# The high-by-low product of the scores as two 64-row matmuls on the two halves of the array

## The chip, the cores and the metric

The kernel runs on one core of a Trainium2 chip. The metric is the device time of one execution, in microseconds (us). The time before is 4194.33 us, the median of three runs (4191.17 to 4195.89).

## What is computed

A layer norm, a ReLU, and a masked attention with 8 heads of 64 columns over 1024 nodes, for 16 images; the input is added at the end. In the reference:

```python
h = jnp.maximum(_layernorm(x, axis=-1), 0.0)          # x: 16 x 1024 x 512, adj: 1024 x 1024
q = (h @ Wq + bq).reshape(b, n, H, HD)                # H = 8, HD = 64; k and v likewise
scores = jnp.einsum('bihd,bjhd->bhij', q, k) / jnp.sqrt(jnp.float32(HD))
mask = jnp.where(adj == 0, jnp.float32(-1000000000.0), jnp.float32(0.0))
weights = jax.nn.softmax(scores + mask[None, None, :, :], axis=-1)
out = x + jnp.einsum('bhij,bjhd->bihd', weights, v).reshape(b, n, H * HD)
```

## The kernel before

Every engine has its own program, written out by hand, and semaphores tie them together. The outer loop runs over 16 images (the first and the last are written out, the 14 between are a hardware loop). In an image, the heads come in 4 pairs; a pair has 32 **units**, a head 16. A unit u takes one column block of 128 keys for a group of 4 row blocks of 128 queries. On TensorE a unit turns 4 blocks of probabilities into PSUM tile T (`turn_probs`, 4 transposes) and multiplies the turned block u-2 by v into O (`contract`, 2 matmuls). On every even unit it also computes one **score block**, 5 blocks ahead (`score`): 128 queries by 1024 keys into S, of which there are two. Image by image that makes 64 score blocks and 128 units.

ScalarE takes T to pT's high part (`probs_hi`), VectorE subtracts for the low part (`probs_low`), for every unit. For every score block VectorE adds the mask and takes the maximum (`shift`, 1024 columns), ScalarE takes the exponential (`exponential`).

All matmuls in float32r drop low bits, so each operand is held as a high and a low part, and a product has three terms. For the scores, the parts of q stand one under the other: for the first head of a pair rows 0 to 63 of qA hold q_high, rows 64 to 127 q_low; for the second head (qB) it is the other way round. k has two planes of 1024 columns, [k_high; k_high] and [k_low; k_low], both with the same 64 rows twice. A score block is then, for each of the two halves of 512 columns, two matmuls over all 128 rows: q times plane 0 (L513) and q times plane 1 (L514). So the second one computes q_high k_low and, along with it, q_low k_low. The second copy of the 64 rows of k comes by DMA (`copy_k`, L233).

Other work is put into given units of the program (the **slots**): the projection of q and k of the next pair, eight pieces of 6 matmuls (L483) at u = 4, 6, 8, 9, 12, 14, 16, 17 of each pair; v of the next image, 12 matmuls each (L496), at u = 121, 123 to 127 and in the first units of the next image; the turning of the next image's normalised input, 4 transposes (L462), at u = 83, 85, 87, 88, 91, 92, 95, 96; and the turning of the output of a group, 4 transposes (L546), at every eighth unit. ScalarE and VectorE take these results from the PSUM bank misc and split them (L654, L664, L772; L669, L762). The first score block of the next pair stands at u = 22.

GpSimd makes k_low (L390), normalises the input tiles (L371) and finishes the outputs: `finish` reads yparts, a copy of misc that ScalarE makes (`copy_y`, L624), and adds to xres.

SyncE issues all DMAs from one queue, in program order, with its waits in between: in every pair the stores and loads of xres, `copy_k` of the first 512 columns, input tiles (xln), `copy_k` of the other 512 columns, the load of the next 1 MB of weights (wqk, L222), and in the third pair of an image behind that six input tiles (L214), each of which waits for the turning of the tile two before it.

Of the kernel before, what the change touches and what calls it, by code (L numbers as in the profile page):

```python
# [81 lines left out]
def some(n):  # L82

    return not (isinstance(n, int) and n <= 0)


def adj_preln_kernel(nc, x, adj, Wq, bq, Wk, bk, Wv, bv, out):
    with ExitStack() as ctx:
# [28 lines left out]
        yparts = sb("yparts", [P, GB, 2, HD])  # L117
# [45 lines left out]
        q_low, k_low, k_copied = sem("q_low"), sem("k_low"), sem("k_copied")  # L163
        v_mm, v_biased, v_hi, v_ready = sem("v_mm"), sem("v_biased"), sem("v_hi"), sem("v_ready")
# [11 lines left out]
        def qk_buffers(pair, second):  # L176


            if not second:
                return qA[:, :], kA[:, :, :]  # L180
            return qB[:, pair % 2, :], kB[:, pair % 2, :, :]

# [27 lines left out]
        def _(sp):  # L210
# [14 lines left out]
            def copy_k(b, p, half):  # L225

                cols = slice(half * HALF, (half + 1) * HALF)

                sp.wait_ge(k_low, 4 * (PAIRS * b + p) + 2 * (half + 1))
                for second in range(2):  # L230
                    _, k = qk_buffers(p, second)
                    own, other = (slice(0, HD), slice(HD, P))[::-1 if second else 1]
                    sp.dma_start(k[other, :, cols].bitcast(F32), k[own, :, cols].bitcast(F32)  # L233
                                 ).then_inc(k_copied, 16)

# [35 lines left out]
            for half in range(2):  # L271
                copy_k(0, 0, half)
            store_wqk(3)
# [11 lines left out]
            def body(b, first=False, last=False):  # L285
                for p in range(PAIRS):
# [24 lines left out]
                    if not (last and p == PAIRS - 1):  # L311
                        copy_k(b, p + 1, 0)
                    if p < len(STATS_SLOTS) and not last:
                        for t in STATS_TILES[p][2:]:
                            sp.wait_ge(bn_done, NB * (b + 1) + t - XLN + 1)
                            load_xln(b + 1, t)
# [5 lines left out]
                    if not (last and p == PAIRS - 1):  # L322
                        copy_k(b, p + 1, 1)
                    if not (last and p >= PAIRS - 2):

                        sp.wait_ge(qk_mm, 4 * (PAIRS * b + p + 1) + 4)
                        load_wqk((p + 2) % PAIRS)
                    if p == len(STATS_SLOTS) - 1 and not last:
                        for t in range(XLN, NB):
                            sp.wait_ge(h_turned, NB * (b + 1) + t - XLN + 1)  # L330
                            load_xln(b + 1, t)
# [123 lines left out]
        def _(pe):  # L455
# [44 lines left out]
            def score(b, s):  # L500
# [6 lines left out]
                pe.wait_ge(k_copied, 64 * (pair + 1))  # L507
                if some(n - 1):
                    pe.wait_ge(exped, n - 1)
                for half in range(2):  # L510
                    cols = slice(half * HALF, (half + 1) * HALF)
                    dst = S[:, s % 2, cols]
                    pe.matmul(dst, q[:, i * P:(i + 1) * P], k[:, 0, cols], start=True, stop=False)  # L513
                    mm = pe.matmul(dst, q[:, i * P:(i + 1) * P], k[:, 1, cols], start=False, stop=True)  # L514
# [96 lines left out]
        def _(act):  # L611
            def copy_out(b, g):
                n = GROUPS * b + g
                act.wait_ge(contracted, NB * (n + 1))
                if some(n):
                    act.wait_ge(o_turned, n)
                act.copy(oT[:], O[:]).then_inc(o_copied, 1)

            def copy_y(b, g):
                n = GROUPS * b + g  # L620
                act.wait_ge(o_turned, n + 1)
                if some(n):
                    act.wait_ge(y_added, n)
                act.copy(yparts[:].rearrange("p i l d -> p (i l d)"), misc[:]).then_inc(y_copied, 1)  # L624
# [268 lines left out]
```

## Time and profile before

| | |
|---|---|
| median of three runs | 4194.33 us |
| the profiled execution: its span | 4186.6 us |
| PE / PEld (matmuls / weight loads) busy | 97% / 81% |
| DVE / ACT / POOL busy | 75% / 75% / 31% |
| granted TensorE clock, mean | 0.998 |

The median is 7.7 us over the span of the profiled execution, which covers the first to the last instruction of the program. "Busy" of a matmul is longer than what it keeps from the next one: matmuls follow each other before the one ahead has ended, so that the distances between starts, in the timeline, are what counts.

### The profile page before, as it was taken

Reading aid. Unit: us, or ns where it says so; the run is one execution under the profiler, and the core shown is the slowest. Engines: PE = TensorE matmul, PEld = TensorE weight load, DVE = VectorE, ACT = ScalarE, POOL = GpSimd, SP = SyncE. Lnnn points to the kernel's source line nnn. Section 1 sums busy time; section 2 is a strip of 40 time slices with the busy share of each in tenths; the row PEclk is TensorE's granted clock in tenths of the full one; section 3 lists DMA queues with packets and bytes.
Section 4 is the critical chain, followed back from the end, with each engine's and each line's share of the span. In section 5 each row is a group of like instructions: output and inputs, shape, how many; then the busy total and the mean of one; then the engine's idle time right before and its main releaser. Section 6 shows DMA issues by size and latency. Waiting matters only on the chain.

```text
span 4186.6 us, 77847 instructions
## 1 busy us (share of the span) xinstructions
PE 4080.4 (97%) x22528; PEld 3370.6 (81%) x22528; DVE 3120.0 (75%) x5128; ACT 3149.6 (75%) x5642; POOL 1287.4 (31%) x1665
## 2 busy tenths in 40 slices
PE   7999999999999999999999999999999999999998
PEld 6888888888787887878878788788887888888887
DVE  6877868778687786777867677676777768767677
ACT  5877868778687786867868688686886868868687
POOL 4233332333323333223333233332332322333222
PEclk9999999999999999999999999999999999999999
DMA  5221212212222221122212122121221212212111
GB/s 176 72 73 56 81 48 75 66 57 83 61 60 67 65 77 59 59 67 76 66 59 71 54 76 66 59 79 47 76 72 54 82 48 71 83 44 83 46 51 31
DMA packets 219598, 282.56 MB, mean 67 GB/s; under 512 B 12305, under 2 KB 143377, under 8 KB 210577
## 3 DMA queue, kind: packets, MB, share of 16 engines
q1 hardware_dynamic: 219152, 277.14, 21.9%
q8 instruction: 217, 3.56, 0.4%
q14 instruction: 229, 1.87, 0.2%
HBM read 172.23 MB, written 37.75 MB: 50 GB/s over the span
## 4 chain that ended last, share of the span: by engine, by line
PE 89%; DVE 4%; issue 3%; ACT 2%; DMA 1%; POOL 1%; DVEq 0%; SPq 0%; POOLq 0%; ACTq 0%
PE O L538 21%; PE T L525 19%; PE misc L483 17%; PE S L513 10%; PE S L514 10%; PE misc L496 8%; PE misc L546 3%; DVE pT L796 2%; PE misc L462 1%; ACT pT L633 1%; DVE qA L772 1%; DMA xln<-in_x 1%; ACT qA L664 1%; DVE S L790 1%; DVE hT L762 0%
## 5 line engine op out<-in xcount | busy, mean ns | idle before, releaser
L796 DVE TENSOR_TENSOR pT<-T,pT 128x512 fp32r<-128x512 f32 x2048 | 1412.4, 690 | 831.1 <-ACT pT L633 808.8
L633 ACT CAST pT<-T 128x512 fp32r<-128x512 f32 x2048 | 1192.7, 589 | 711.0 <-PE T L525 676.1
L538 PE MATMUL O<-pT,vs 128*128 128x512 f32 x4096 | 1366.0, 415 | 60.0 <-DVE pT L796 46.0
L790 DVE CUSTOM_DVE_ANT_0 S<-S,mask 128x1024 f32<-128x1024 f32 x1024 | 1252.3, 1223 | 5.9 <-PE S L514 4.3
L525 PEld LDWEIGHTS T<-ident,probs 128*128 128x128 f32 x8192 | 1013.9, 140 | 258.4 <-ACT probs L641 0.3
L525 PE MATMUL T<-ident,probs 128*128 128x128 f32 x8192 | 1210.1, 272 | 0.0
L641 ACT ACTIVATE probs<-S,negmax 128x1024 f32<-128x1024 f32 x1024 | 1152.6, 1126 | 8.5 <-DVE negmax L790 5.3
L538 PEld LDWEIGHTS O<-pT,vs 128*128 128x128 f32 x4096 | 690.9, 189 | 178.2 <-DVE pT L796 70.4
L483 PE MATMUL misc<-hT,wqk 128*128 128x512 f32 x3036 | 789.1, 395 | 0.0
L483 PEld LDWEIGHTS misc<-hT,wqk 128*128 128x128 f32 x3036 | 560.6, 188 | 120.3
L400 POOL TENSOR_TENSOR yparts<-yparts 128x256 f32<-128x256 f32 x256 | 188.7, 737 | 1043.9 <-ACT yparts L624 1043.2
L513 PE MATMUL S<-kA,qA 128*128 128x512 f32 x1024 | 447.2, 437 | 3.9 <-ACT probs L641 3.2
L513 PE MATMUL S<-kB,qB 128*128 128x512 f32 x1024 | 447.0, 436 | 0.0
L514 PE MATMUL S<-kA,qA 128*128 128x512 f32 x1024 | 403.3, 394 | 0.0
L514 PE MATMUL S<-kB,qB 128*128 128x512 f32 x1024 | 402.3, 393 | 0.0
L496 PE MATMUL misc<-wv,hT 128*128 128x512 f32 x1476 | 363.8, 395 | 0.4 <-issue 0.4
L377 POOL TENSOR_TENSOR vs<-proj,vs 128x512 fp32r<-128x512 f32 x128 | 168.2, 1314 | 543.4 <-ACT vs L679 543.4
L496 PEld LDWEIGHTS misc<-wv,hT 128*128 128x128 f32 x1476 | 271.2, 188 | 65.8 <-issue 6.5
L654 ACT ACTIVATE proj<-misc,bqk 128x512 f32<-128x512 f32 x253 | 174.4, 689 | 182.7 <-PE misc L483 182.7
L390 POOL TENSOR_TENSOR kA<-proj,kA 64x512 fp32r<-64x512 f32 x128 | 164.5, 1285 | 474.9 <-ACT kB L664 474.9
L513 PEld LDWEIGHTS S<-kA,qA 128*128 128x128 f32 x1024 | 193.9, 189 | 27.2 <-issue 5.7
L514 PEld LDWEIGHTS S<-kA,qA 128*128 128x128 f32 x1024 | 195.2, 191 | 21.4
(68 smaller groups left out, 3333.0 us busy)
## 6 DMA issues: line engine op xcount, KB each, us to landing
wqk<-wqk_split SPq DMA_DIRECT2D x63, 1024.0 KB, 7.0
xln<-in_x SPq DMA_DIRECT2D x240, 256.0 KB, 3.7
xres<-in_x SPq DMA_DIRECT2D x66, 512.0 KB, 3.7
kA<-kA SPq DMA_DIRECT2D x128, 256.0 KB, 3.2
kB<-kB SPq DMA_DIRECT2D x128, 256.0 KB, 3.7
out<-xres SPq DMA_DIRECT2D x64, 512.0 KB, 3.2
probs<-in_adj SPq DMA_DIRECT2D x4, 1024.0 KB, 5.1
wqk_split<-vs SPq DMA_DIRECT2D x3, 1024.0 KB, 11.0
```

The source lines that it names most:

```text
L400: gp.tensor_tensor(y, y, yparts[:, :, 1], ALU.add).then_inc(y_summed, 1)
L483: mm = pe.matmul(bank, wqk[:, w, c, wl, :], hT[:, hl, c, cols], start=n == 0, stop=n == len(parts) - 1)
L496: mm = pe.matmul(bank, hT[:, hl, c, j * P:(j + 1) * P], wv[:, wl, c, :], start=n == 0, stop=n == len(parts) - 1)
L513: pe.matmul(dst, q[:, i * P:(i + 1) * P], k[:, 0, cols], start=True, stop=False)
L514: mm = pe.matmul(dst, q[:, i * P:(i + 1) * P], k[:, 1, cols], start=False, stop=True)
L525: mm = pe.transpose(T[:, u % 2, i * P:(i + 1) * P], probs[:, (GB * g + i) % RING, j * P:(j + 1) * P], ident[:])
L538: mm = pe.matmul(O[:], vs[:, j, head, :], pT[:, u % PT, part, :], start=(j == 0 and part == 0), stop=(j == NB - 1 and part == 1))
L633: act.copy(pT[:, u % PT, 0, :], T[:, u % 2, :]).then_inc(p_hi, 1)
L641: act.activation(probs[:, s % RING, :], S[:, s % 2, :], ACT.Exp, bias=negmax[:, s % RING:s % RING + 1], scale=-1.0, accum_out=rowsum[:, s ...
L654: act.activation(proj[:, k % 2], bank, ACT.Identity, bias=bqk[:, w, p % PAIRS:p % PAIRS + 1], scale=-SCALE if w == 0 else 1.0).then_inc(qk ...
L790: dve.tensor_tensor_reduce(S[:, s % 2, :], S[:, s % 2, :], mask[:, s % NB, :], 1.0, 3.0e38, ALU.add, ALU.min, negmax[:, s % RING:s % RING ...
L796: dve.tensor_tensor(pT[:, u % PT, 1, :], T[:, u % 2, :], pT[:, u % PT, 0, :].bitcast(F32), ALU.subtract).then_inc(p_lo, 1)
```

## The change

1. For each score block the two matmuls q times plane 0 stay as they are, now both in front. In place of the two 128-row matmuls q times plane 1 stand two matmuls over 64 rows, q_high times k_low: for columns 0 to 511 on rows 0 to 63, for columns 512 to 1023 on rows 64 to 127 (two halves of the array, two PSUM banks). The product q_low k_low is no longer computed.
2. The half that lies on the rows on which q_high does not stand needs a copy of q_high there. `copy_q` makes it by DMA in four pieces of 64 x 512 for every pair: for row blocks 0 to 3 into the plane-1 rows of k that became free, for row blocks 4 to 7 into a new tile, qdup.
3. `copy_k` leaves out the copies of plane 1 that nobody reads: two of its four DMAs in a pair carry one plane, two carry both.
4. qdup gets its room from yparts, which is now the tile oT: `copy_out` (O to oT) waits until GpSimd has finished with the group before (y_added), not for the turning alone.
5. `score` waits for three of the four q copies too; for the last one (second head, row blocks 4 to 7) only where it is read. That copy waits, on SyncE, for the pair's last score block, and the other waits of copy_q are on ScalarE's high parts.

On TensorE a score block and what surrounds it, in the first image. Before (S is the tile of scores, T of turned probabilities, O of the contraction):

```order
L525 MATMUL T<-ident,probs 128x128 x4
L538 MATMUL O<-pT,vs 128x512 x2
L525 MATMUL T<-ident,probs 128x128 x4
L513 MATMUL S<-kB,qB 128x512
L514 MATMUL S<-kB,qB 128x512
L513 MATMUL S<-kB,qB 128x512
L514 MATMUL S<-kB,qB 128x512
L483 MATMUL misc<-hT,wqk 128x512 x6
```

The same place now:

```order
L573 MATMUL T<-ident,probs 128x128 x4
L586 MATMUL O<-pT,vs 128x512 x2
L573 MATMUL T<-ident,probs 128x128 x4
L555 MATMUL S<-kB,qB 128x512 x2
L562 MATMUL S<-kB 128x512
L562 MATMUL S<-kB,qB 128x512
L522 MATMUL misc<-hT,wqk 128x512 x6
```

The number of matmuls is the same; the two of plane 0 stand together, and the two of L562 are the 64-row ones (the sizes printed are those of the output).

On SyncE's queue, the third pair of an image in the loop, from the second half of the k copies on. Before:

```order
L233 DMA kA<-kA 64x2x512 [waits k_low]
L233 DMA kB<-kB 64x2x512
L222 DMA wqk<-wqk_split 128x2048 [waits qk_mm]
L214 DMA xln<-in_x 128x512 [waits h_turned] x6
L239 DMA out<-xres 128x8x128 [waits y_added]
```

Now:

```order
L247 DMA kA<-kA 64x2x512 [waits k_low]
L247 DMA kB<-kB 64x512
L256 ISA
L265 DMA qdup<-qA 64x512 [waits qk_high]
L235 DMA wqk<-wqk_split 128x2048 [waits qk_mm]
L256 REGISTER_ALU
L264 REGISTER_ALU [waits qk_high]
L265 DMA qdup<-qB 64x512 [waits scored]
L227 DMA xln<-in_x 128x512 [waits h_turned] x6
```

The load of the weights stands behind the copy out of qA and its wait, and the six input tiles behind the copy out of qB with two waits.

The diff:

```diff
--- before.py
+++ after.py
@@ -114,7 +114,8 @@
         bv_all = sb("bv_all", [P, D])
         bqk = sb("bqk", [P, 2, PAIRS])
         ident = sb("ident", [P, P])
-        yparts = sb("yparts", [P, GB, 2, HD])
+        yparts = oT[:].rearrange("p (i l d) -> p i l d", i=GB, l=2)
+        qdup = sb("qdup", [P, HALF], F32R)
         negmax = sb("negmax", [P, RING])
         rowsum = sb("rowsum", [P, 2 * RING])
         rinv = sb("rinv", [P, 2, GB])
@@ -161,6 +162,7 @@
         h_turned, h_hi, h_lo = sem("h_turned"), sem("h_hi"), sem("h_lo")
         qk_mm, qk_evac, qk_high = sem("qk_mm"), sem("qk_evac"), sem("qk_high")
         q_low, k_low, k_copied = sem("q_low"), sem("k_low"), sem("k_copied")
+        q_copied, q_copied_last = sem("q_copied"), sem("q_copied_last")
         v_mm, v_biased, v_hi, v_ready = sem("v_mm"), sem("v_biased"), sem("v_hi"), sem("v_ready")
         scored, shifted, exped = sem("scored"), sem("shifted"), sem("exped")
         turned, p_hi, p_lo, contracted = sem("turned"), sem("p_hi"), sem("p_lo"), sem("contracted")
@@ -179,6 +181,17 @@
             if not second:
                 return qA[:, :], kA[:, :, :]
             return qB[:, pair % 2, :], kB[:, pair % 2, :, :]
+
+        def q_again(pair, second, i):
+
+
+            rows = slice(HD, P) if not second else slice(0, HD)
+            at = i % GB * P
+            if i >= GB:
+                return qdup[rows, at:at + P]
+            _, k = qk_buffers(pair, second)
+            at += HALF if second else 0
+            return k[rows, 1, at:at + P]
 
         def x_tile(b, t):
 
@@ -230,8 +243,27 @@
                 for second in range(2):
                     _, k = qk_buffers(p, second)
                     own, other = (slice(0, HD), slice(HD, P))[::-1 if second else 1]
-                    sp.dma_start(k[other, :, cols].bitcast(F32), k[own, :, cols].bitcast(F32)
+                    planes = slice(0, 2 if half != second else 1)
+                    sp.dma_start(k[other, planes, cols].bitcast(F32), k[own, planes, cols].bitcast(F32)
                                  ).then_inc(k_copied, 16)
+
+            def copy_q(b, p, second, half):
+
+
+                pair = PAIRS * b + p
+                q, k = qk_buffers(p, second)
+                own, other = (slice(0, HD), slice(HD, P))[::-1 if second else 1]
+                sp.wait_ge(qk_high, 2 * (4 * pair + 2 * half + 1) + 1 + second)
+                sp.sem_inc(sp_passed)
+                src = q[own, half * HALF:(half + 1) * HALF]
+                if half == 0:
+                    dst = k[other, 1, second * HALF:(second + 1) * HALF]
+                else:
+                    dst = qdup[other, :]
+                    if second and some(pair):
+                        sp.wait_ge(scored, 16 * pair)
+                sp.dma_start(dst.bitcast(F32), src.bitcast(F32)
+                             ).then_inc(q_copied_last if second and half else q_copied, 16)
 
             def store(b, p):
                 sp.sem_inc(sp_passed)
@@ -270,6 +302,8 @@
             store_wqk(2)
             for half in range(2):
                 copy_k(0, 0, half)
+                for second in range(2):
+                    copy_q(0, 0, second, half)
             store_wqk(3)
             store_wqk(0)
             sp.wait_ge(h_turned, NB)
@@ -310,6 +344,8 @@
                                 load_xres(b, p + 1)
                     if not (last and p == PAIRS - 1):
                         copy_k(b, p + 1, 0)
+                        for second in range(2):
+                            copy_q(b, p + 1, second, 0)
                     if p < len(STATS_SLOTS) and not last:
                         for t in STATS_TILES[p][2:]:
                             sp.wait_ge(bn_done, NB * (b + 1) + t - XLN + 1)
@@ -321,10 +357,13 @@
                             load_xln(b + 1, t)
                     if not (last and p == PAIRS - 1):
                         copy_k(b, p + 1, 1)
+                        copy_q(b, p + 1, 0, 1)
                     if not (last and p >= PAIRS - 2):
 
                         sp.wait_ge(qk_mm, 4 * (PAIRS * b + p + 1) + 4)
                         load_wqk((p + 2) % PAIRS)
+                    if not (last and p == PAIRS - 1):
+                        copy_q(b, p + 1, 1, 1)
                     if p == len(STATS_SLOTS) - 1 and not last:
                         for t in range(XLN, NB):
                             sp.wait_ge(h_turned, NB * (b + 1) + t - XLN + 1)
@@ -505,13 +544,22 @@
                 pair = PAIRS * b + s // 16
                 pe.wait_ge(q_low, 4 * pair + 3 + (s // 8) % 2)
                 pe.wait_ge(k_copied, 64 * (pair + 1))
+                pe.wait_ge(q_copied, 48 * (pair + 1))
+                second = (s // 8) % 2
+                if second and i >= GB:
+                    pe.wait_ge(q_copied_last, 16 * (pair + 1))
                 if some(n - 1):
                     pe.wait_ge(exped, n - 1)
                 for half in range(2):
                     cols = slice(half * HALF, (half + 1) * HALF)
-                    dst = S[:, s % 2, cols]
-                    pe.matmul(dst, q[:, i * P:(i + 1) * P], k[:, 0, cols], start=True, stop=False)
-                    mm = pe.matmul(dst, q[:, i * P:(i + 1) * P], k[:, 1, cols], start=False, stop=True)
+                    pe.matmul(S[:, s % 2, cols], q[:, i * P:(i + 1) * P], k[:, 0, cols],
+                              start=True, stop=False)
+                for half in range(2):
+
+
+                    cols, rows = slice(half * HALF, (half + 1) * HALF), slice(half * HD, half * HD + HD)
+                    q_hi = q[rows, i * P:(i + 1) * P] if half == second else q_again(s // 16, second, i)
+                    mm = pe.matmul(S[:, s % 2, cols], q_hi, k[rows, 1, cols], start=False, stop=True)
                 mm.then_inc(scored, 1)
 
             def turn_probs(b, u):
@@ -610,18 +658,17 @@
         @block.scalar
         def _(act):
             def copy_out(b, g):
+
                 n = GROUPS * b + g
                 act.wait_ge(contracted, NB * (n + 1))
                 if some(n):
-                    act.wait_ge(o_turned, n)
+                    act.wait_ge(y_added, n)
                 act.copy(oT[:], O[:]).then_inc(o_copied, 1)
 
             def copy_y(b, g):
                 n = GROUPS * b + g
                 act.wait_ge(o_turned, n + 1)
-                if some(n):
-                    act.wait_ge(y_added, n)
-                act.copy(yparts[:].rearrange("p i l d -> p (i l d)"), misc[:]).then_inc(y_copied, 1)
+                act.copy(oT[:], misc[:]).then_inc(y_copied, 1)
 
             def probs_hi(b, u):
                 n = UNITS * b + u
```

## Rows read from the trace of the kernel before

**Rows 1.** The head of the page: the span, each engine's busy time and number of instructions.

```profile
span 4186.6 us, 77847 instructions
PE 4080.4 (97%) x22528; PEld 3370.6 (81%) x22528; DVE 3120.0 (75%) x5128; ACT 3149.6 (75%) x5642; POOL 1287.4 (31%) x1665
```

**Rows 2.** The page's chain of work that ended last, by engine.

```profile
PE 89%; DVE 4%; issue 3%; ACT 2%; DMA 1%; POOL 1%; DVEq 0%; SPq 0%; POOLq 0%; ACTq 0%
```

**Rows 3.** Groups by form, the whole program: count, busy us, mean ns, idle before.

```profile
L514 PE MATMUL S<-kA,qA 128*128 128x512 f32 x1024 | 403.3, 394 | 0.0
L514 PEld LDWEIGHTS S<-kA,qA 128*128 128x128 f32 x1024 | 195.2, 191 | 21.4
```

**Rows 4.** Timeline of PE, one score block: start us, duration us.

```profile
2003.37 0.48 PE L513 MATMUL S<-kA,qA 128*128 128x512 f32 x1
2003.69 0.40 PE L514 MATMUL S<-kA,qA 128*128 128x512 f32 x1
2003.92 0.39 PE L513 MATMUL S<-kA,qA 128*128 128x512 f32 x1
2004.15 0.39 PE L514 MATMUL S<-kA,qA 128*128 128x512 f32 x1
2004.38 0.62 PE L538 MATMUL O<-pT,vs 128*128 128x512 f32 x2
```

**Rows 5.** Timeline of PEld, the weight loads of the same block.

```profile
2003.35 0.19 PEld L513 LDWEIGHTS S<-kA,qA 128*128 128x128 f32 x1
2003.46 0.19 PEld L514 LDWEIGHTS S<-kA,qA 128*128 128x128 f32 x1
2003.69 0.19 PEld L513 LDWEIGHTS S<-kA,qA 128*128 128x128 f32 x1
```

**Rows 6.** Busy us of each engine in five stretches of one image.

```profile
core 0: us, PE busy (x) PEld busy (x) DVE busy (x) ACT busy (x) POOL busy (x), PEclk, DMA share, GB/s
1979.25:1986.58 7.33, 6.62 (x41) 5.36 (x40) 5.43 (x7) 6.58 (x12) 2.67 (x4) 1.00 0.67 211
1992.04:2003.37 11.33, 11.33 (x71) 9.59 (x70) 10.14 (x18) 9.86 (x19) 2.10 (x3) 1.00 0.01 1
2007.00:2037.05 30.05, 30.05 (x165) 25.04 (x164) 21.80 (x37) 22.81 (x41) 10.71 (x15) 1.00 0.25 71
2044.98:2065.16 20.18, 19.45 (x125) 16.10 (x124) 19.20 (x35) 17.39 (x32) 6.70 (x9) 1.00 0.22 71
2109.36:2138.94 29.58, 28.58 (x144) 23.06 (x142) 15.32 (x26) 12.56 (x23) 8.51 (x8) 1.00 0.01 3
```

**Rows 7.** Timeline of PE at a pair's end: its wait, the next pair's first block.

```profile
1984.35 0.60 PE L525 MATMUL T<-ident,probs 128*128 128x128 f32 x4
1985.66 0.73 PE L538 MATMUL O<-pT,vs 128*128 128x512 f32 x2 [0.71 <-DVE pT L796]
1986.58 0.48 PE L513 MATMUL S<-kA,qA 128*128 128x512 f32 x1
```

**Rows 8.** ACT's last high part for that block, and landings of DMAs (page).

```profile
1981.84 0.62 ACT L664 CAST qA<-proj 64x512 fp32r<-64x512 f32 x1
...
wqk<-wqk_split SPq DMA_DIRECT2D x63, 1024.0 KB, 7.0
...
kA<-kA SPq DMA_DIRECT2D x128, 256.0 KB, 3.2
```

**Rows 9.** Timelines at the end of an image's third pair: SP, ACT, PE, POOL, PE.

```profile
2038.78 0.67 SPq L222 DMA_DIRECT2D wqk<-wqk_split  x1
...
2040.67 0.34 SPq L214 DMA_DIRECT2D xln<-in_x  x1
...
2039.64 0.62 ACT L664 CAST qA<-proj 64x512 fp32r<-64x512 f32 x1
...
2041.95 0.40 PE L514 MATMUL S<-kB,qB 128*128 128x512 f32 x1
...
2046.66 1.52 POOL L371 TENSOR_SCALAR xln<-xln,negmean,rstd 128x512 f32<-128x512 f32 x2 [3.33 <-DMA xln<-in_x]
...
2047.49 0.66 PE L462 MATMUL misc<-ident,xln 128*128 128x128 f32 x4 [0.43 <-POOL xln L371]
```

**Rows 10.** One group's last step on POOL, the next copy of O on ACT.

```profile
2024.65 1.29 POOL L411 TENSOR_TENSOR xres<-xres,yparts 128x256 f32<-128x256 f32 x1 [0.17 <-POOL yparts L403]
...
2035.06 0.59 ACT L617 COPY oT<-O 128x512 f32<-128x512 f32 x1 [0.33 <-PE O L538]
```

## The prediction

> **What bounds the kernel now.** I read the head of the page first, then the chain, then the timeline of TensorE for the distances between starts, then the busy times of stretches. The head shows TensorE busy for 97% of the span, VectorE and ScalarE for 75% each [rows 1]; the chain that ended last lies on TensorE for 89% of its length [rows 2]. The matmuls' mean duration of 394 ns [rows 3] is not what one costs: in the timeline the starts of the four matmuls of a score block and of the contraction behind it lie 0.32, 0.23, 0.23 and 0.23 us apart [rows 4]. So a 512-column matmul costs 0.23 us, or 0.92 for the block's four, the excess of the first belonging to its weights, which load behind the transposes. The weight load of the next matmul starts when the one ahead starts, and lasts 0.19 us, under the 0.23 [rows 4, 5]: it is hidden, one ahead.
>
> The average hides that not every stretch has the same limit. An image has 64 score blocks. Five stretches show what the other engines would do if TensorE were faster [rows 6]:
>
> - 7 blocks with projection pieces (2007.00 to 2037.05): TensorE 30.05 of 30.05 us, VectorE 21.80, ScalarE 22.81. TensorE alone. 28 such blocks in an image, 7 in each pair.
> - 4 blocks without them (1992.04 to 2003.37): TensorE 11.33 of 11.33, but VectorE 10.14 and ScalarE 9.86. There is room for 1.19 us at most, that is 0.30 for a block. Two of the four pairs have 6 such blocks, 12 in an image.
> - v's pieces (2109.36 to 2138.94, 4 blocks): VectorE 15.32 of 29.58. TensorE alone, but for one wait of 1 us; I count 5 of that pair's 6 blocks.
> - 6 blocks with the turning of the input (2044.98 to 2065.16): VectorE is busy 19.20 of 20.18 us. Nearly full already.
> - a pair's end (1979.25 to 1986.58): TensorE is behind, with a wait of 0.71 us for VectorE's low part [rows 7]. VectorE and ScalarE catch up here with the splits of q and k. 3 blocks in each pair, 12 in an image.
>
> **The change part by part.** *The two matmuls.* Removed per block: two matmuls at 0.23, 0.46 us. Added: two 64-row matmuls on different rows of the array and different banks. No row of this trace has a 64-row matmul or two matmuls at once, so the price is bounded. Best case: they stream together, 0.23 for both, and the gain is 0.23. Serial: 0.46, gain 0. Worst: TensorE has to empty at the change from 128 to 64 rows and back. A matmul's end lies 0.394 - 0.23 = 0.16 us behind the start of the next [rows 3, 4], so emptying twice costs 0.33; if the weights can't load ahead either, 0.19 more each time [rows 5], 0.71 in all. The pair then costs between 0.56 and 0.94, and the change loses between 0.10 and 0.48 us per block. I take concurrent, with 0.03 us for the second to start (the first score weight load and its matmul start 0.02 apart [rows 4, 5]): 0.26, a gain of **0.20 us per block**. The nearest row for the weights is the hidden, one-ahead load; here each of the two loads fills only its own rows.
>
> The Trainium skill speaks on both sides of this. "TensorE: Matmul & The Clock Gate", Part 3, says that matmuls in different row groups start about 4 ns apart and run at once; by that the pair costs 0.23 and the block gains 0.23. "TensorEngine Tiling (Array Packing)", Key Properties, says "Changing tiling mode (not just tile) drains the TensorE". The change switches twice per block, 2048 times in all, and the page gives no price. No row here shows either.
>
> *What of 0.20 arrives.* Stretches of TensorE alone: 28 + 5 blocks, 6.6 us per image. The 12 plain ones: 4 x 0.20 = 0.80 of the 1.19 us of room; VectorE would then be busy 10.14 of 10.53 us, and the engines hand over to each other with only two units between, so I count 80%: 1.9 us. The 6 blocks with the input's turning: 0.98 us of room, I count 0.6. The 12 at the pairs' ends: nothing, the wait only grows. Sum 9.1 us per image, 16 images: **146 us** (205 if all 1024 blocks gained).
>
> *SyncE's queue.* Four q copies are added in a pair, each 128 KB, and two of the 128 KB planes of the k copies go. DMA engines are far from full in all stretches but the pair's end (share 0.67) [rows 6]. The issues (about 0.65 us each, as the weights' [rows 9]) and their waits are what counts, on everything behind them. In front of the pair's next block stands the third q copy: ScalarE makes the high part by 1982.46, a copy takes 3.2 us, so it lands at about 1985.7; the block starts at 1986.58 [rows 7, 8]. It holds by 0.9 us, and both ends hang on the same engines: nothing. The fourth copy is needed 12 blocks into the pair: nothing. The stores and loads of xres and the input tiles for the statistics stand many microseconds off their use: nothing.
>
> In the third pair it is different. Now the weights' load is issued at 2038.78 and the third input tile's at 2040.67; the tile comes behind the 1 MB of weights, GpSimd waits 3.33 us for it until 2046.66, and TensorE waits for GpSimd until 2047.49 [rows 9]. With the change the copy out of qA waits for the high part, done at 2040.26, so the weights are issued at about 2040.9 in place of 2038.78 and land, at 7.0 us [rows 8], at 2047.9. Behind it the copy out of qB waits for the pair's last score block, whose matmuls end at 2042.3 [rows 9]; the tile goes out at 2042.9 and lands right behind the weights, at about 2048.6 in place of 2046.4. TensorE stands in order in front of that turning: **2.0 us** in each of 15 images, 30 us. It can't be hidden by more than the little that VectorE has left to do; I keep 15 to 35.
>
> *yparts in oT.* The next copy of O now waits for GpSimd's last step. That ends at 2025.94, the copy starts at 2035.06 [rows 10]: 9 us of cover, and there is none of it lost with blocks 0.2 us shorter. Nothing. The start of the program has three more small copies in front of the first block: 1 us.
>
> **Sum.** 146 - 30 - 1 = 115 us off the profiled execution's 4186.6, 4071 us of span; the median lies 7.7 above the span: 4079 us. I give 4078.
>
> **Rivals.**
>
> 1. *Concurrent, but not for free.* One weight load or a short gap stays open, and a block gains 0.05 to 0.12 us. For it: the first matmul behind the transposes already shows 0.09 us of open weight load [rows 4, 5]. At 0.09 the plain stretches have room for all of it and some 52 blocks of an image gain: 75 - 31 = 44 us, 4150.
> 2. *TensorE empties at each switch* (slower). The mechanism: the 128-row matmul must leave the array before the 64-row pair may start, and the pair before the contraction. Price: 0.10 us lost per block; nearly all blocks pay, less what the waits at the pairs' ends swallow, 85% of 102 us, and the 30 of the queue: 4311. With weights open as well 0.48 us: about 4640. It decides from a cost of 0.08 us per switch, where the pair costs 0.42 and its gain no longer pays the 30 us. For it: none of the 22528 matmuls in the trace is of another height, so the kernel never paid this. Against: the trace's changes between transposes and multiplications cost only the weight load. The Trainium skill's drain rule, named above, is this rival.
> 3. *The halves don't run at once.* The pair stays at 0.46: no gain, 30 us from the queue, 4225. For it: all starts in the trace are in single file.
> 4. *The third q copy comes late.* The cover of 0.9 us is gone when TensorE is faster or a copy meets the other transfers (share 0.67 there). Some 1 us in each of 64 pairs: 4143.
>
> **How the numbers follow.** Forecast 0.47, partial concurrency 0.25 (of it 0.04 within 0.2% of before), emptying 0.18, no concurrency 0.06, late copies 0.04. The range reaches from 4020 (0.23 a block nearly all arriving, and a small queue cost) to 4240 (no concurrency and the upper queue cost): it leaves out the emptying. The forecast's own range is 4020 to 4105 (0.17 a block, and 35 us for the queue). A measurement of this kernel tells about 0.2%, 8 us, from no change. Faster: 0.47 + 0.21 + 0.04 = 0.72; same 0.04; slower 0.24.
>
> **What the profile after would show.** The starts of the two 64-row matmuls within 0.05 us of each other, and the next start 0.23 behind: forecast. Starts 0.1 to 0.2 apart: rival 1. A gap ahead of the first and behind the second, with the weight loads waiting: rival 2. In a block-by-block view, the 7 blocks with projections take 28.65 in place of 30.05 us, the 4 plain ones about 10.7 in place of 11.33, and a pair's end stays at 7.3 with a longer wait for VectorE. The third input tile's turning comes about 2 us later relative to the third pair's last score block, with the wait put down to GpSimd and the DMA. The most likely way to be wrong is the price of the pair, which no row shows.

## Result: 4% slower, by a fixed price for each change of the array's height

The changed kernel takes 4361.72 us (median of 4 runs, 4357.32 to 4363.39), the kernel before in the same comparison 4192.75 us. The ratio is 1.040, with a 95% interval of 1.039 to 1.042: 169 us more, where 115 us less was forecast. The time lies outside the range of 4020 to 4240. It is what rival 2 described. The granted clock was 0.997 in the profiled execution, for 0.998 before; by estimate that is 4 us at most of the 169.

The page of the changed kernel, its head, its chain by engine, and the two largest groups of the new matmuls:

```profile
span 4360.2 us, 78818 instructions
PE 4259.5 (98%) x22528; PEld 3100.6 (71%) x22528; DVE 3127.2 (72%) x5128; ACT 3157.4 (72%) x5642; POOL 1287.0 (30%) x1665
...
PE 91%; issue 2%; DVE 2%; DMA 2%; ACT 1%; POOL 1%; SPq 0%; DVEq 0%; POOLq 0%; ACTq 0%
...
L562 PE MATMUL S<-kA,qA 64*128 64x512 f32 x512 | 254.4, 497 | 0.0
...
L562 PEld LDWEIGHTS S<-kA,qA 64*128 64x128 f32 x512 | 94.1, 184 | 186.4 <-issue 186.4
```

Who waited for whom in the changed kernel (us in total, times, longest), for the loads of the new matmuls:

```profile
PEld S L562 <- issue: 370.4, 1024, 0.7
```

TensorE is busy 179 us longer with as many matmuls as before [rows 1]. VectorE and ScalarE do what they did. A 64-row matmul shows 497 ns, where the 128-row one in its place showed 394 [rows 3]. And the weight loads, hardly ever idle for "issue" before, now have idle time in front of the first 64-row load of each of the 1024 pairs, 0.36 us in the mean.

The timeline of TensorE for one score block and what follows it (start us, duration us), the counterpart of [rows 4]:

```profile
2104.45 0.71 PE L555 MATMUL S<-kB,qB 128*128 128x512 f32 x2
2105.09 0.49 PE L562 MATMUL S<-kB 64*128 64x512 f32 x1
2105.10 0.50 PE L562 MATMUL S<-kB,qB 64*128 64x512 f32 x1
2105.52 0.73 PE L586 MATMUL O<-pT,vs 128*128 128x512 f32 x2
2106.09 0.60 PE L594 MATMUL misc<-ident,oT 128*128 128x128 f32 x4
```

The weight loads of the same block, the counterpart of [rows 5]:

```profile
2104.42 0.30 PEld L555 LDWEIGHTS S<-kB,qB 128*128 128x128 f32 x2
2105.09 0.18 PEld L562 LDWEIGHTS S<-kB 64*128 64x128 f32 x1 [0.37 <-issue]
2105.09 0.18 PEld L562 LDWEIGHTS S<-kB,qB 64*128 64x128 f32 x1
2105.52 0.30 PEld L586 LDWEIGHTS O<-pT,vs 128*128 128x128 f32 x2 [0.24 <-issue]
```

The two 64-row matmuls do run at once: they start 0.01 us apart at most. But three distances have grown. From the first 128-row matmul to the pair it is 0.64 us, for two matmuls that took 0.55 (0.32 + 0.23, [rows 4]). From the pair to the next start it is 0.42, not 0.23. And the first two matmuls behind the pair take 0.57 us until the next start; in the run with full height below, the same two take 0.45. The weight loads tell why: neither the pair's weights nor those of the first matmul behind it are loaded ahead. Each load starts with its own matmul, where before it started with the one ahead (except behind the transposes, where the load and its matmul already started together, [rows 4, 5]). One block is no accident: over nearly all of the 1024 blocks in the two traces the median distances are 0.32 to 0.33 in front of the pair, 0.42 to 0.43 from the pair to the next start, and 0.34 from that start to the one behind it, where full height shows 0.23, 0.46 (for the two) and 0.23.

The stretches of [rows 6], the same units of the program, in the changed kernel (stretch, its length, busy us by engine):

```profile
2061.74:2069.24 7.50, 6.96 (x41) 4.82 (x40) 5.44 (x7) 6.58 (x12) 2.49 (x4) 1.00 0.54 151
2074.86:2086.88 12.02, 12.02 (x72) 8.52 (x70) 10.28 (x18) 9.99 (x20) 2.08 (x3) 1.00 0.01 1
2090.68:2122.03 31.35, 31.35 (x166) 23.17 (x164) 21.80 (x37) 22.80 (x41) 10.89 (x15) 1.00 0.27 73
2130.13:2151.66 21.53, 20.07 (x125) 14.67 (x124) 19.60 (x35) 17.37 (x32) 6.71 (x9) 1.00 0.28 86
```

In the order of [rows 6]: a pair's end 7.50 for 7.33 (2 blocks), the plain stretch 12.02 for 11.33 (4 blocks), the projections 31.35 for 30.05 (7 blocks), the input's turning 21.53 for 20.18 (6 blocks), v's pieces 30.69 for 29.58 (4 blocks; 0.3 of it a longer stop that the profile puts down to "issue", 1.32 us for 1.00). In the plain stretch and the projections, where TensorE is alone, that is 0.17 and 0.19 us more for a block, and half of that at a pair's end. There the wait for VectorE gives some back:

```profile
2067.17 0.60 PE L573 MATMUL T<-ident,probs 128*128 128x128 f32 x4
2068.32 0.73 PE L586 MATMUL O<-pT,vs 128*128 128x512 f32 x2 [0.55 <-DVE pT L843]
2069.24 0.71 PE L555 MATMUL S<-kA,qA 128*128 128x512 f32 x2
```

From the transposes to the next pair's first block it is 2.07 us, for 2.23 before [rows 7]: the wait has become shorter by what TensorE lost.

The stretch with the input's turning has a second cause. SyncE's queue and TensorE at the third tile, in the changed kernel, the counterpart of [rows 9]:

```profile
2126.01 0.59 SPq L235 DMA_DIRECT2D wqk<-wqk_split  x1
2127.51 0.47 SPq L265 DMA_DIRECT2D qdup<-qB  x1
2128.16 1.66 SPq L227 DMA_DIRECT2D xln<-in_x  x2
...
2133.82 0.66 PE L501 MATMUL misc<-ident,xln 128*128 128x128 f32 x4 [1.46 <-POOL xln L410]
```

TensorE waits 1.46 us there, for 0.43 before. GpSimd's start on the tile, and what the page says of the weights' load (median us from issue to landing):

```profile
2133.00 1.52 POOL L410 TENSOR_SCALAR xln<-xln,negmean,rstd 128x512 f32<-128x512 f32 x2 [4.52 <-DMA xln<-in_x]
```

```profile
wqk<-wqk_split SPq DMA_DIRECT2D x63, 1024.0 KB, 5.7
```

Counted from GpSimd's start on the tile before (2127.28, and 2042.13 in the kernel before), the third tile is issued 2.3 us later than before and GpSimd starts on it 1.2 us later: its wait is 4.52 us for 3.33. The rest is made up by the load of the weights ahead of it, which lands 5.7 us behind its issue, for 7.0 before [rows 8]. No run shows why it is faster now.

### The profile page after: what moved, and what is told of

It reads as the page before. It is cut to its first block, busy times and chain, and to the rows that moved or that the text cites. A ratio compares the mean times of both kernels' runs of the same rounds, so it can differ in the third digit from the quotient of the medians.

```text
span 4360.2 us, 78818 instructions
## 1 busy us (share of the span) xinstructions
PE 4259.5 (98%) x22528; PEld 3100.6 (71%) x22528; DVE 3127.2 (72%) x5128; ACT 3157.4 (72%) x5642; POOL 1287.0 (30%) x1665
## 4 chain that ended last, share of the span: by engine, by line
PE 91%; issue 2%; DVE 2%; DMA 2%; ACT 1%; POOL 1%; SPq 0%; DVEq 0%; POOLq 0%; ACTq 0%
PE O L586 23%; PE T L573 19%; PE misc L522 18%; PE S L555 10%; PE S L562 9%; PE misc L535 8%; PE misc L594 3%; DMA xln<-in_x 2%; PE misc L501 1%; DVE pT L843 1%; ACT pT L680 1%; DVE qA L819 1%; ACT qA L711 1%; POOL xln L410 0%; POOL vs L461 0%
## 5 line engine op out<-in xcount | busy, mean ns | idle before, releaser
L586 PE MATMUL O<-pT,vs 128*128 128x512 f32 x4096 | 1430.7, 430 | 45.4 <-DVE pT L843 29.0
L522 PE MATMUL misc<-hT,wqk 128*128 128x512 f32 x3036 | 839.4, 412 | 0.0
L586 PEld LDWEIGHTS O<-pT,vs 128*128 128x128 f32 x4096 | 648.9, 189 | 249.4 <-issue 116.4
L439 POOL TENSOR_TENSOR oT<-oT 128x256 f32<-128x256 f32 x256 | 188.3, 736 | 1127.7 <-ACT oT L671 1127.7
L555 PE MATMUL S<-kA,qA 128*128 128x512 f32 x1024 | 365.4, 438 | 4.8 <-ACT probs L688 2.6
L555 PE MATMUL S<-kB,qB 128*128 128x512 f32 x1024 | 361.8, 434 | 0.0
L562 PE MATMUL S<-kA,qA 64*128 64x512 f32 x512 | 254.4, 497 | 0.0
L562 PE MATMUL S<-kB,qB 64*128 64x512 f32 x512 | 252.7, 493 | 0.0
L562 PEld LDWEIGHTS S<-kA,qA 64*128 64x128 f32 x512 | 94.1, 184 | 186.4 <-issue 186.4
L666 ACT COPY oT<-O 128x512 f32<-128x512 f32 x256 | 150.6, 588 | 100.3 <-PE O L586 100.3
```

What stands on the lines that cost most here:

```text
L439: gp.tensor_tensor(y, y, yparts[:, :, 1], ALU.add).then_inc(y_summed, 1)
L522: mm = pe.matmul(bank, wqk[:, w, c, wl, :], hT[:, hl, c, cols], start=n == 0, stop=n == len(parts) - 1)
L555: pe.matmul(S[:, s % 2, cols], q[:, i * P:(i + 1) * P], k[:, 0, cols], start=True, stop=False)
L562: mm = pe.matmul(S[:, s % 2, cols], q_hi, k[rows, 1, cols], start=False, stop=True)
L586: mm = pe.matmul(O[:], vs[:, j, head, :], pT[:, u % PT, part, :], start=(j == 0 and part == 0), stop=(j == NB - 1 and part == 1))
```

## The experiments

**Everything but the height.** The changed kernel, with this in `score`:

```diff
-                    mm = pe.matmul(S[:, s % 2, cols], q_hi, k[rows, 1, cols], start=False, stop=True)
+                    mm = pe.matmul(S[:, s % 2, cols], q[:, i * P:(i + 1) * P], k[:, 0, cols], start=False, stop=True)
```

> Part of the computation is changed: the last two matmuls of a score block run over all 128 rows and read plane 0 of k once more, in place of q_high times k_low on 64 rows. Everything else of the changed kernel stays: the q copies, the queue of SyncE, yparts in oT, the new waits, the order of the matmuls. Theory A (the change of height on TensorE costs the time): the block is back at four matmuls of 0.23 us, and only the queue's cost is left, about 0.8 us in each of 15 images by the longer wait in front of the third input tile's turning: 4200 to 4210 us. Theory B (copies, queue or the shared tile cost it): stays over 4300. My prediction before the result had 30 us for the queue: 4223.

4205.8 us (4200.8 to 4213.7, 5 runs); ratio to the kernel before 1.0038 (1.0025 to 1.0052). Of the 169 us, 156 are gone with the height alone. The copies, their waits, the shared tile and the matmuls' order together cost 15, known to some 5 us: the five runs spread with the granted clock, from 4200.8 us at 0.999 to 4213.7 at 0.996. Its timeline at the same place in the program as above:

```profile
2043.64 0.71 PE L555 MATMUL S<-kB,qB 128*128 128x512 f32 x2
2044.19 0.63 PE L561 MATMUL S<-kB,qB 128*128 128x512 f32 x2
2044.66 0.62 PE L585 MATMUL O<-pT,vs 128*128 128x512 f32 x2
2045.11 0.60 PE L593 MATMUL misc<-ident,oT 128*128 128x128 f32 x4
```

1.47 us from the block's start to the transposes, for 1.64 with the pair: 0.17 us, made of +0.09 in front of the pair, -0.05 for the pair itself with what follows it (0.42 for 0.47), and +0.12 behind.

**The queue's order on top.** In the third pair the weights' load goes ahead of the third q copy, and the third and fourth input tiles ahead of the fourth:

```diff
-                        copy_q(b, p + 1, 0, 1)
+                        if p != len(STATS_SLOTS) - 1:
+                            copy_q(b, p + 1, 0, 1)
...
                         load_wqk((p + 2) % PAIRS)
-                    if not (last and p == PAIRS - 1):
-                        copy_q(b, p + 1, 1, 1)
+                    if p == len(STATS_SLOTS) - 1:
+                        copy_q(b, p + 1, 0, 1)
                     if p == len(STATS_SLOTS) - 1 and not last:
                         for t in range(XLN, NB):
                             sp.wait_ge(h_turned, NB * (b + 1) + t - XLN + 1)
                             load_xln(b + 1, t)
+                            if t == XLN + 1:
+                                copy_q(b, p + 1, 1, 1)
+                    elif not (last and p == PAIRS - 1):
+                        copy_q(b, p + 1, 1, 1)
```

> As the run with full height (plane 0 read again over 128 rows), and in the third pair SyncE issues the weights' load ahead of the third q copy, and the third and fourth input tiles ahead of the fourth q copy. If the queue's order is what is left of the cost, this comes back to the kernel before, 4190 to 4196 us. If the copies themselves cost (transfers, issues), it stays at the time of the run with full height.

4187.4 us (11 runs); ratio 0.9991 (0.9982 to 1.0000). All of the 15 us come back, and a little more. So the copies, their transfers and the shared tile cost nothing that shows in the sum: what was left was the order of the queue. The waits for GpSimd's normalised tile tell it (who waits for whom, us in total, times, longest). In the run with full height alone:

```profile
PEld misc L501 <- POOL xln L410: 39.5, 38, 2.7
PE misc L501 <- POOL xln L410: 26.9, 15, 2.5
```

With the queue's order changed as well:

```profile
PEld misc L506 <- POOL xln L415: 10.4, 23, 0.5
```

Of the matmuls' waits at the turning, 26.9 us for GpSimd and 4.5 for VectorE, 12.1 us are left, all for VectorE; in the kernel before they were 10.4 and 7.2. The third q copy, which now goes out later, was waited for three times, 3.6 us in all.

The same move in the complete changed kernel:

> The changed kernel, complete, with SyncE's order in the third pair changed: the weights' load ahead of the third q copy, the third and fourth input tiles ahead of the fourth. At full height the same move took the time from 4206 to 4187 us. Theory A (the change of height costs the rest): 12 to 19 us off 4362, 4343 to 4350 us, still some 150 us over the kernel before. If the queue had more to do with the loss than the full-height runs show, below 4330.

4345.0 us (4 runs); ratio 1.037 (1.035 to 1.039). That is 17 us less than the changed kernel and still 155 over the one before.

**One matmul less.** This measures the step that decides how much of a saving on TensorE arrives. In the kernel before:

```diff
-                    pe.matmul(dst, q[:, i * P:(i + 1) * P], k[:, 0, cols], start=True, stop=False)
-                    mm = pe.matmul(dst, q[:, i * P:(i + 1) * P], k[:, 1, cols], start=False, stop=True)
+                    mm = pe.matmul(dst, q[:, i * P:(i + 1) * P], k[:, 0, cols], start=True, stop=half == 1)
+                    if half == 0:
+                        pe.matmul(dst, q[:, i * P:(i + 1) * P], k[:, 1, cols], start=False, stop=True)
```

> The kernel before with one of the four matmuls of a score block left out (q times plane 1 for columns 512 to 1023). No copies, no 64-row matmuls. It tests the step that counted how much of 0.23 us saved per block arrives: by the stretches of the prediction 0.23 in 33 of 64 blocks, most of it in 12 plain ones, 0.6 us in the 6 with the input's turning, nothing at the pairs' ends: 10.3 us per image, 4193 - 165 = 4028 us. If all arrives: 3958. If VectorE and ScalarE hold it back more: over 4070.

4026.2 us (4 runs); ratio 0.961 (0.959 to 0.962), 165 us less. The stretches agree (pair's end, plain, projections):

```profile
1902.60:1909.83 7.23, 6.44 (x40) 4.93 (x38) 5.45 (x7) 6.46 (x12) 2.90 (x4) 1.00 0.65 199
1915.19:1925.92 10.73, 10.73 (x68) 8.61 (x66) 9.93 (x18) 9.73 (x19) 2.08 (x3) 1.00 0.01 2
1929.35:1957.82 28.47, 28.47 (x158) 23.72 (x157) 21.70 (x37) 22.69 (x41) 10.77 (x16) 1.00 0.26 75
```

7 blocks with projections give 1.58 us, the full 0.23 each; 4 plain ones 0.60, 0.15 each, less than the 0.18 that I counted; the pair's end gives 0.10 for two blocks, where I counted nothing. The two misses have opposite signs, so the exact sum is in part luck.

**A second pair at the same height.** The pair is issued twice in every block:

```diff
+                for half in range(2):
+                    cols, rows = slice(half * HALF, (half + 1) * HALF), slice(half * HD, half * HD + HD)
+                    q_hi = q[rows, i * P:(i + 1) * P] if half == second else q_again(s // 16, second, i)
+                    mm = pe.matmul(S[:, s % 2, cols], q_hi, k[rows, 1, cols], start=False, stop=True)
```

> The changed kernel with the pair of 64-row matmuls issued twice in each block (the term q_high k_low counts double). Theory A (a cost per change of height, and none within one height): the second pair costs one matmul's 0.23 us, 1024 x 0.23 x 0.85 to 1.0 = 200 to 235 us on top of 4362: 4560 to 4600 us, and its weights load ahead. Theory C (every 64-row pair costs 0.42 us from start to the next start): 1024 x 0.42 on top: about 4790 us.

4580.9 us (2 runs), 219 us over the changed kernel, 0.21 per block. (The kernel before, run beside this experiment and the next three, took 4187.5 us, 5 less than beside the changed kernel; their differences from 4361.7 are known to no more than that.) Timelines of TensorE and of its weight loads:

```profile
2108.63 0.49 PE L562 MATMUL S<-kA,qA 64*128 64x512 f32 x1
2108.63 0.49 PE L562 MATMUL S<-kA 64*128 64x512 f32 x1
2108.96 0.39 PE L566 MATMUL S<-kA,qA 64*128 64x512 f32 x1
2108.97 0.39 PE L566 MATMUL S<-kA 64*128 64x512 f32 x1
2109.29 0.74 PE L590 MATMUL O<-pT,vs 128*128 128x512 f32 x2
```

```profile
2108.63 0.18 PEld L562 LDWEIGHTS S<-kA,qA 64*128 64x128 f32 x1 [0.37 <-issue]
2108.74 0.19 PEld L566 LDWEIGHTS S<-kA,qA 64*128 64x128 f32 x1
```

This splits the 0.42 us. From the first pair to the second, with no change between them, it is 0.33: 0.23 of columns and 0.10 because the first pair's weights are not there. From the second pair, whose weights were loaded behind the first's start (at 2108.74), to the 128-row matmul it is 0.32 to 0.33: 0.23 and some 0.10 for leaving. Theory C, a 64-row pair that is slow in itself, is out.

**Three pairs and no 128-row matmul in the block.**

```diff
-                for half in range(2):
-                    cols = slice(half * HALF, (half + 1) * HALF)
-                    pe.matmul(S[:, s % 2, cols], q[:, i * P:(i + 1) * P], k[:, 0, cols],
-                              start=True, stop=False)
+                for turn in range(2):
+                    for half in range(2):
+                        cols = slice(half * HALF, (half + 1) * HALF)
+                        at = half * HD
+                        pe.matmul(S[:, s % 2, cols], q[at:at + HD, i * P:(i + 1) * P],
+                                  k[at:at + HD, 0, cols], start=turn == 0, stop=False)
```

> The changed kernel with all of a score block as three pairs of 64-row matmuls: the two 128-row matmuls of plane 0 are replaced by two pairs (columns 0 to 511 on rows 0 to 63, columns 512 to 1023 on rows 64 to 127, so that parts of the products are missing and others double). One change of height into the block, now from the transposes, and one out, as before. Theory A: 3 x 0.23 plus the same two changes, about 1.16 us for the block as in the changed kernel: 4340 to 4385 us. Theory C: 3 x 0.42: about 4650 us.

4365.5 us (2 runs), the changed kernel's time within what can be told. Its timeline:

```profile
2107.47 0.60 PE L575 MATMUL T<-ident,probs 128*128 128x128 f32 x4
2108.00 0.73 PE L557 MATMUL S<-kB,qB 64*128 64x512 f32 x4
2108.57 0.40 PE L564 MATMUL S<-kB,qdup 64*128 64x512 f32 x1
2108.57 0.39 PE L564 MATMUL S<-kB,qB 64*128 64x512 f32 x1
2108.90 0.50 PE L522 MATMUL misc<-hT,wqk 128*128 128x512 f32 x1
```

Two pairs in place of the two 128-row matmuls cost the same as these: 0.57 us for the first two, then 0.33 with the change out. The first 64-row start now lies 0.53 us behind the transposes' start, where a 128-row one lies 0.35 behind; so entering costs from the transposes too: 0.18 us in front of the start, and 0.10 for the pair's own weights (0.33 from the first pair to the second), against the 0.09 of open weights that a 128-row matmul pays behind the transposes. Net of that it is 0.19 us, as from a multiplication (0.09 + 0.10). A block that has to do both changes costs the same whichever of its matmuls are 64 rows high. A complete kernel of this form was not tried: in it both halves of the array would have to add into the same columns of S, and no run here shows what that takes.

**Both on one half of the array.**

```diff
-                    cols, rows = slice(half * HALF, (half + 1) * HALF), slice(half * HD, half * HD + HD)
+                    cols, rows = slice(half * HALF, (half + 1) * HALF), slice(second * HD, second * HD + HD)
```

(and q read from the same rows of q)

> The changed kernel with both 64-row matmuls on the same half of the array, the one where q_high stands (for one of the two halves of columns the k_low rows read there are those that the changed kernel uses for the q copy in one quarter, so that term is wrong). If the two run at once because they lie on different halves, they now run one behind the other, 0.23 us apart: 1024 x 0.23 x 0.85 to 1.0 on top of 4362: 4560 to 4600 us. If the chip never ran them at once: 4362.

4564.4 us (2 runs), 203 us over the changed kernel:

```profile
2105.50 0.73 PE L561 MATMUL S<-kA,qA 64*128 64x512 f32 x2
2106.16 0.73 PE L585 MATMUL O<-pT,vs 128*128 128x512 f32 x2
```

Now it is 0.66 us from the first 64-row start to the next 128-row start. On two halves the same work takes 0.42, so the concurrency is worth its full 0.23 us. What the change promised on this point is there.

**Fewer columns.**

```diff
-                    mm = pe.matmul(S[:, s % 2, cols], q_hi, k[rows, 1, cols], start=False, stop=True)
+                    short = slice(half * HALF, half * HALF + HALF // 2)
+                    mm = pe.matmul(S[:, s % 2, short], q_hi, k[rows, 1, short], start=False, stop=True)
```

> The changed kernel with the two 64-row matmuls over 256 columns each (half of the term q_high k_low is left out). Theory A1 (the 0.42 us from the pair's start to the next start is 0.21 us of columns and 0.2 us of emptying and weights, one behind the other): the distance falls by 0.107 to 0.31 us, 4255 to 4275 us. Theory A2 (a fixed time that the columns hide): the distance stays at 0.42 us, 4362 us.

4257.2 us (2 runs), 104 less. The distance to the next start falls to 0.31:

```profile
2105.51 0.38 PE L563 MATMUL S<-kB 64*128 64x256 f32 x1
2105.51 0.38 PE L563 MATMUL S<-kB,qB 64*128 64x256 f32 x1
2105.82 1.66 PE L522 MATMUL misc<-hT,wqk 128*128 128x512 f32 x6
```

0.11 us less for 256 columns less. The other 0.2 us stays, and the columns do not hide it.

**Every second block.**

```diff
+                    if s % 2:
+                        mm = pe.matmul(S[:, s % 2, cols], q[:, i * P:(i + 1) * P], k[:, 0, cols], start=False, stop=True)
+                        continue
```

> The changed kernel with the 64-row pair only in every second score block; in the others the last two matmuls run over all 128 rows and read plane 0 of k once more (there the term q_high k_low is replaced by a second q k_high). Theory A, a fixed price per block with a pair: half way between 4206 (none) and 4362 (all), 4280 to 4288 us. If a change of height has an effect beyond its own block (other engines, later stalls), it is off that line by more than 10 us.

4288.3 us (4280.5 to 4294.0, 4 runs); the middle between none (4205.8) and all (4361.7) is 4283.8. The 4.5 us between them lie within the spread of the runs, which goes with the granted clock: 4280.5 us at 0.998, 4294.0 at 0.995. So no effect beyond the block shows: the price belongs to the block that pays it.

**A change that the queue suggested.** The kernel before, complete, with the weights' load of the third pair behind the fourth input tile:

```diff
+                    late = p == len(STATS_SLOTS) - 1 and not last
-                    if not (last and p >= PAIRS - 2):
+                    if not (last and p >= PAIRS - 2) and not late:
...
                             load_xln(b + 1, t)
+                            if t == XLN + 1:
+                                sp.wait_ge(qk_mm, 4 * (PAIRS * b + p + 1) + 4)
+                                load_wqk((p + 2) % PAIRS)
```

> The kernel before, complete, with one move: in the third pair of an image the 1 MB load of the weights is issued behind the third and fourth input tiles in place of ahead of them. If TensorE's wait at the third tile's turning (0.7 us per image before) is only the tile standing behind the weights, it goes: up to 15 us less, 4178 to 4188 us. If something else holds the turning (GpSimd, VectorE), no change: 4193.

4187.4 us (11 runs), 4191.2 for the kernel before; ratio 0.9991 (0.9982 to 1.0000). That is 4 us where up to 15 were expected, at the edge of what can be told. TensorE's waits for GpSimd's tile are nearly gone:

```profile
PEld misc L466 <- POOL xln L375: 7.9, 15, 0.5
```

22.1 and 10.4 us were put down to it in the kernel before (weight loads and matmuls). Most of the wait was cover for VectorE, which is busy 19.20 of 20.18 us there [rows 6] and now ends last more often: the matmuls' wait for it rose from 7.2 us (25 times) to 13.9 (45 times). Together 17.6 us of the matmuls' waits became 13.9, which is the 4 us. By 0.1% it is the fastest complete version here.

## Why the prediction was wrong

- **What bounds the kernel: right.** TensorE alone in most stretches, 0.23 us for a 512-column matmul, its weights loaded one ahead.
- **The price of the pair: wrong; this is the step that failed.** I took 0.26 us, a gain of 0.20 per block. The pair itself is what I took it for: its two matmuls start together, and on one half they cost 0.23 more. What failed is the step that chose among the bounds: it put the emptying at nothing, though no row showed a change of height, and took the hidden load that runs one ahead as the nearest row for the weights. That row shows two matmuls of one height. Across a change of height no load ran ahead, in either direction. The changes cost, all read from the distances above: about 0.09 us entering, 0.10 for the pair's own weights, 0.09 to 0.10 leaving, and 0.11 for the weights of the first matmul behind. Together 0.40 us per block, for 0.23 saved: 0.17 lost in place of 0.20 gained. The four sizes are measured; which of them is emptying and which weights is my reading of where the loads start.
- **The bounds: right.** I had 0.10 to 0.48 us lost for this case. Emptying costs less than the 0.16 us that I took from a matmul's duration less its distance, the open weights less than the 0.19 of a load's duration. A load's distance from the next, 0.11 us in [rows 5], was the better row: the four terms are all about that long, though no run shows why.
- **How much arrives: right.** 165 us were expected of one matmul less, 165 came, in part by luck, since the plain blocks gave less and the pairs' ends more than I counted. For a loss the same table holds in reverse: nearly everything arrives where TensorE is alone, and the pairs' ends take half.
- **SyncE's queue: right in place and in the chain of waits, twice too large.** I had 2.0 us per image; it was 1.0, 15 us in all. The issues came as late as I had them, 2.3 us for the tile; the term that was too large is the landing, which I kept at the 7.0 us of before and which was 5.7. The third q copy, the copies' transfers and the shared tile cost nothing in the sum, as said: with the queue in the other order the whole package is at 0.9991 of the kernel before.
- **The chances.** Rival 2 had 0.18. It named the mechanism, the four terms, and the point from which it decides: 0.08 us per change; it was 0.20. With the measured 0.17 lost in each of 1024 blocks, 90% of it arriving, and 15 us for the queue, its sum gives 4193 + 157 + 15 = 4365; the 90% is fitted to the result, and with the 85% and the 30 us on record it would be 4371. The trace of before had no row for a change of height, and 2048 of them were to be added. For an operation that the kernel has never paid and then pays in every block, I should have given the worse half of its bounds more weight.

The Trainium skill, "TensorEngine Tiling (Array Packing)", Key Properties, says that a change of tiling mode drains the TensorE. The traces agree that a change costs, and give it a price here: 0.2 us for each, half of it in weights that are not loaded ahead. They do not show the array empty: the pair starts 0.07 us ahead of the end that the profile gives for the matmuls in front of it (2105.09, for 2104.45 + 0.71), where within one height it is 0.16. The Trainium skill, "TensorE: Matmul & The Clock Gate", Part 3, says that matmuls on different row groups run at once, starts about 4 ns apart. The traces agree (0.01 us or less). The first outweighs the second as long as there is one pair for every two changes.

## What to carry to other kernels

Two half-height matmuls at once save one matmul's time per pair (0.23 us here at 512 columns), and a round trip between full and half height costs 0.40 us. So, by an estimate from these numbers that no run here tested as a gain, there must be at least two pairs between two changes before anything is gained, and with two it is 0.06 us; put such work together in long runs, or leave the array at one height. When a change promises to take work off a bound engine, first leave that work out and measure what arrives; then put the copies and the queue in without the new instruction. The two runs together show what the instruction itself may cost.

## What was not expected of the hardware

- Within one height the weights of a half-height pair load ahead, onto the rows that are in use: the second pair's load started at 2108.74, 0.11 us behind the first pair's start, and where the weights are loaded ahead a pair costs 0.23 us (with three pairs, 0.57 from the first to the third, 0.33 of it the first). Across heights nothing is loaded ahead, though the program's order is the same.
- A change costs nearly the same from transposes as from a multiplication: with three pairs the block took 4365.5 us in all for 4361.7, though its entry is from the transposes.
- What a pair costs beyond its columns (its own weights, and leaving half height) is 0.2 us with 256 columns as with 512: 0.31 and 0.42 us to the next start. A longer matmul does not hide it.
